# One attention-and-FFN kernel: x loaded already transposed and normalised in that layout

## The chip, the cores and the metric

One core of a Trainium2 chip runs the whole program. The metric is the device time of one execution in microseconds; the figure quoted for a kernel is the median of its runs. Engines are named as in the profile: PE is TensorE, DVE VectorE, ACT ScalarE, POOL GpSimd, SP the engine that issues the DMAs here. Each takes its own instructions strictly in the order in which the program gives them, and waits on semaphores.

## What is computed

Two sandwich blocks on x of 8 x 512 x 1024 (batch, position, feature), float32: attention with 8 heads of 64 over its layer-normalised input, then a 1024 x 1024 linear layer with a routed low-rank part. Cut to what matters:

```
x = x + layernorm(attn(layernorm(x)))
x = x + layernorm(ffn(layernorm(x)))

attn:  qkv = x @ w_qkv.T + b_qkv            # (b, 512, 1536): q, k, v
       scores = einsum('bhfc,bhtc->bhft', k, q), masked where f > t with -10000
       vals = softmax over f, times v
       out = vals @ w_o.T + b_o
ffn:   hidden @ W.T + b + (x @ A[:r].T @ B[:, :r].T of the best of 4 ranks by a gate)
layernorm(x) = (x - mean(x)) / sqrt(var(x) + 1e-5), over the 1024 features
```

Only the first layernorm and what feeds the q, k and v projections is touched.

## The kernel before

Matrix products that matter to accuracy are done in split form: an operand is rounded to a high part (names ending in h, written by ACT) and a low part (names ending in l, written by DVE as the difference), and a product is three matmuls: high by high, high by low, low by high.

The program has two phases, attention and output; each is written out engine by engine. In the attention phase the weights wh and wl stay in SBUF, and a loop runs over batches 0 to 6, with batch 7 written out behind it. A batch has ten slots, h = 0 to 9. In slot h stand the scores of head h (L797; for heads 3 to 6, the list AHEAD, at the end of the slot before), its masking and maxima (L504 on DVE) and exponentials (L662 on ACT), the normalisation of its probabilities (L381 on POOL), and, one slot later, the transposes of these (L816 on PE) with their high and low copies (p_hi L629 on ACT, p_lo L471 on DVE); in slot h + 2 come the values (L841 on PE), then their sum (L530) and store. Projections fill the rest: q and k for two heads at a time ("pair", 24 matmuls of 512 columns), v for 128 positions at a time. The table BETWEEN (L104) writes by hand which projections stand in which of the two parts of a slot; FIRST and SECOND are halves of the eight blocks of 128 features.

A projection needs x with features on the partitions, xTh and xTl, eight blocks of 128 x 512. Before the change they are made one batch ahead, in slots 4 to 6: SP loads four tiles of 128 positions (L286), DVE takes mean and variance (L452), POOL normalises a tile in place (L368), PE transposes it in 8 pieces of 128 x 128 into two PSUM banks (L756), ACT evicts the high part (x_hi, L622) and DVE the low one (x_lo, L464). These 32 transposes share the two banks ps_j with the projections. After them come k and q of pair 0 and pair 1 of the next batch, in slots 6 to 9.

SP issues every DMA: the x tiles, the duplicate of k to the other half of the partitions (dup_k, L288), the store of a head's values (L294). PE waits for xTl before pair 0 (L780), for the bank to be free (L750), for the exponentials of the head before (L807), for p_lo (L821, L844).

Of the kernel before, what the change touches and what calls it, by code (L numbers as in the profile page):

```python
# [16 lines left out]
ALU = mybir.AluOpType  # L17
ACT = mybir.ActivationFunctionType
AX = mybir.AxisListType
F32 = mybir.dt.float32  # L20
# [57 lines left out]
def attention_phase(nc, x, wqkvT, bqk, bv, valsT, vals_stored, ps_o, W, woT, bo, wagT, BT):  # L78
# [24 lines left out]
    WHOLE, FIRST, SECOND = range(KD), range(KD // 2), range(KD // 2, KD)  # L103
    BETWEEN = [  # L104
# [18 lines left out]
    EARLY = [("x", t, g) for t in range(NT) for g in range(2)] + [("k", 0), ("q", 0), ("k", 1), ("q", 1)]  # L123
    NOW = [("v", 0), ("v", 1), ("v", 2), ("v", 3), ("k", 2), ("q", 2), ("k", 3), ("q", 3)]

    with ExitStack() as ctx:
# [10 lines left out]
        xs = sb("xs", [P, 3, D], F32)  # L137
# [28 lines left out]
        nmean = sb("nmean", [P, 2], F32)  # L166
        mhalf = sb("mhalf", [P, 1], F32)
# [25 lines left out]
        xn_ready = sem("xn_ready")  # L193
        t_full = [sem(f"t_full{i}") for i in range(2)]
# [40 lines left out]
        xf = x.rearrange("b s d -> (b s) d")  # L235
        vf = valsT.rearrange("b c t -> (b c) t")
# [12 lines left out]
        def x_tile(t, b):  # L249
            if t == 3 and isinstance(b, int) and b == 0:  # L250
                return x3
            return xs[:, t % 3, :]

        def x_bank(t, g, b):

            return (ps_t if isinstance(b, int) and b == 0 and t % 2 else ps_j)[g]
# [7 lines left out]
        def j_index(entry, b):  # L264

            if entry in EARLY:
                return 20 * b + EARLY.index(entry)
            return 20 * b + len(EARLY) + NOW.index(entry)

# [3 lines left out]
        def j_uses(entry, b):  # L273

            return 10 * b + j_index(entry, 0) // 2 + 1
# [8 lines left out]
        def _(sp):  # L284
            def load_x(t, b):
                sp.dma_start(x_tile(t, b)[:, :], xf[bass.ds(b * S + t * P, P), :]).then_inc(x_landed[t], 16)  # L286
# [20 lines left out]
            def body(b, last):  # L307
                if not last:

                    sp.wait_ge(j_lo, j_index(("x", 3, 1), b) + 1)  # L310
                    for t in range(3):
                        load_x(t, b + 1)
                for h in range(SLOTS):
                    if h >= 2:
# [3 lines left out]
                    if h == 4 and not last:  # L318

                        sp.wait_ge(j_full[1], j_uses(("x", 0, 1), b + 1))  # L320
                        load_x(3, b + 1)
# [26 lines left out]
            for t in range(3):  # L348
                load_x(t, 0)
            load_x(3, 0)  # L350
# [16 lines left out]
        def _(pool):  # L367
            def layernorm(t, b):  # L368

                n, q = 4 * b + t, t % 2  # L370
                pool.wait_ge(mv_ready, n + 1)
                pool.tensor_tensor(var_eps[:, q:q + 1], mv[:, q, 1:2], eps[:, :], ALU.add).then_inc(ve_done, 1)
                pool.tensor_tensor(nmean[:, q:q + 1], mv[:, q, 0:1], mone[:, :], ALU.mult)
                pool.wait_ge(ve_done, n + 1)
                pool.tensor_tensor(rstd[:, q:q + 1], var_eps[:, q:q + 1], mhalf[:, :], ALU.pow)
                pool.drain()
                at = x_tile(t, b)[:, :]
                pool.tensor_scalar(at, at, nmean[:, q:q + 1], rstd[:, q:q + 1], ALU.add, ALU.mult)\
                    .then_inc(xn_ready, 1)

            def normalise(h, b):  # L381
# [1004 lines left out]
```

## Time and profile before

| what | value |
|---|---|
| median of 3 runs | 1586.88 us (1586.53 to 1590.59) |
| profiled execution, span | 1589.1 us |
| PE busy in the span | 1500.4 us, 94% |
| DVE, ACT, POOL busy | 975.6, 675.2, 557.7 us |
| mean granted clock of PE | 0.982 |

The attention phase ends at about 921 us of the span, the output phase follows. A batch of the loop takes about 110 us (43.14 to 814.79 us for seven). The clock is given as a share of 2.4 GHz; 0.5 is 1.2 GHz. PE's matmuls overlap, so the pitch from one start to the next is what they cost in a row, and the duration shown is longer.

### The profile page before, as it was taken

Reading aid. Unit: us, or ns where it says so; the run is one execution under the profiler, and the core shown is the slowest. Engines: PE = TensorE matmul, PEld = TensorE weight load, DVE = VectorE, ACT = ScalarE, POOL = GpSimd, SP = SyncE. Lnnn points to the kernel's source line nnn. Section 1 sums busy time; section 2 is a strip of 40 time slices with the busy share of each in tenths; the row PEclk is TensorE's granted clock in tenths of the full one; section 3 lists DMA queues with packets and bytes.
Section 4 is the critical chain, followed back from the end, with each engine's and each line's share of the span. In section 5 each row is a group of like instructions: output and inputs, shape, how many; then the busy total and the mean of one; then the engine's idle time right before and its main releaser. Section 6 shows DMA issues by size and latency. Waiting matters only on the chain. (4 is left out here: it accounts for less than half of the span.)

```text
span 1589.1 us, 24982 instructions
## 1 busy us (share of the span) xinstructions
PE 1500.4 (94%) x8032; PEld 1316.6 (83%) x8032; DVE 975.6 (61%) x2133; ACT 675.2 (42%) x1464; POOL 557.7 (35%) x1099
## 2 busy tenths in 40 slices
PE   7989999989999999999899769999999999999996
PEld 5878878878878788788787569999999999999996
DVE  7475574665665655755745666666666666666663
ACT  5354364464553653644544543333333333333331
POOL 2232431432332323314312444443333334433333
PEclk9999999999999999999999889999999999999998
DMA  6121112012022111120110632211111111111210
GB/s 225 54 54 42 54 40 76 20 36 76 20 53 59 50 40 59 36 79 17 40 37 24 205 97 67 66 66 64 61 64 60 64 62 64 59 64 66 66 60 40
DMA packets 45774, 98.72 MB, mean 62 GB/s; under 512 B 4912, under 2 KB 21296, under 8 KB 45744
## 3 DMA queue, kind: packets, MB, share of 16 engines
q1 hardware_dynamic: 45744, 98.35, 20.2%
q8 instruction: 16, 0.26, 0.1%
q14 instruction: 14, 0.11, 0.0%
HBM read 56.39 MB, written 25.17 MB: 51 GB/s over the span
## 5 line engine op out<-in xcount | busy, mean ns | idle before, releaser
L1312 PE MATMUL ps_f<-wagh,x2Th 128*128 128x364 f32 x768 | 256.1, 333 | 4.4 <-DVE f L1174 2.9
L1312 PE MATMUL ps_f<-wagl,x2Th 128*128 128x364 f32 x768 | 253.9, 331 | 0.0
L1312 PE MATMUL ps_f<-wagh,x2Tl 128*128 128x364 f32 x768 | 253.3, 330 | 0.0
L782 PE MATMUL ps_o<-xTh,wh 128*128 128x512 f32 x504 | 202.2, 401 | 5.5 <-DVE xTl L468 5.5
L782 PE MATMUL ps_o<-xTh,wl 128*128 128x512 f32 x504 | 198.5, 394 | 0.0
L782 PE MATMUL ps_o<-xTl,wh 128*128 128x512 f32 x504 | 198.0, 393 | 0.0
L1312 PEld LDWEIGHTS ps_f<-wagh,x2Th 128*128 128x128 f32 x768 | 146.5, 191 | 6.8 <-issue 5.0
L1312 PEld LDWEIGHTS ps_f<-wagl,x2Th 128*128 128x128 f32 x768 | 145.7, 190 | 1.3
L1312 PEld LDWEIGHTS ps_f<-wagh,x2Tl 128*128 128x128 f32 x768 | 145.2, 189 | 0.0
L392 POOL TENSOR_SCALAR pr<-pr,rden 128x128 f32<-128x128 f32 (+3 forms) x256 | 136.5, 552 | 0.0
L385 POOL TENSOR_TENSOR cw<-wm,cnt 128x4 f32<-128x4 f32 x64 | 12.7, 199 | 346.1 <-ACT pr L668 346.1
L668 ACT ACTIVATE pr<-ps_s,nm 128x128 f32<-128x128 f32 (+3 forms) x256 | 130.5, 520 | 0.1
L1045 POOL TENSOR_TENSOR var_eps<-mv,eps 128x1 f32<-128x1 f32 x95 | 19.0, 200 | 309.0 <-DVE mv L1108 309.0
L1159 DVE TENSOR_TENSOR x2Tl<-ps_x,x2Th 128x512 fp32r<-128x512 f32 x64 | 42.7, 688 | 128.5 <-ACT x2Th L1233 128.3
L474 DVE TENSOR_TENSOR PTl<-ps_t,PTh 128x512 fp32r<-128x512 f32 (+1 forms) x192 | 109.2, 596 | 19.6 <-ACT PTh L632 16.8
L1213 ACT ACTIVATE zf<-f,shift,rstd 128x512 f32<-128x512 f32 x64 | 48.7, 809 | 168.2 <-POOL shift L1049 168.2
L632 ACT ACTIVATE PTh<-ps_t 128x512 fp32r<-128x512 f32 (+1 forms) x192 | 94.3, 527 | 56.4 <-PE ps_t L837 53.7
L665 ACT ACTIVATE wm<-nm,masked 128x3 f32<-128x3 f32 x64 | 19.0, 296 | 233.0 <-DVE nm L524 233.0
L782 PEld LDWEIGHTS ps_o<-xTh,wh 128*128 128x128 f32 x504 | 95.9, 190 | 24.6 <-DVE xTl L468 6.8
L782 PEld LDWEIGHTS ps_o<-xTh,wl 128*128 128x128 f32 x504 | 95.5, 190 | 21.0
L782 PEld LDWEIGHTS ps_o<-xTl,wh 128*128 128x128 f32 x504 | 96.0, 190 | 18.4
L519 DVE TENSOR_REDUCE nm<-ps_s 128x1 f32<-128x128 f32 (+3 forms) x256 | 107.7, 482 | 2.2
(152 smaller groups left out, 3519.4 us busy)
## 6 DMA issues: line engine op xcount, KB each, us to landing
kst<-kst SPq DMA_DIRECT2D x64, 256.0 KB, 3.5
xt<-in_x SPq DMA_DIRECT2D x32, 512.0 KB, 4.1
out<-outs SPq DMA_DIRECT2D x32, 512.0 KB, 3.0
xs<-in_x SPq DMA_DIRECT2D x31, 512.0 KB, 4.4
valsT<-vt SPq DMA_DIRECT2D x64, 128.0 KB, 2.3
vraw<-valsT SPq DMA_DIRECT2D x32, 256.0 KB, 4.3
raw<-in_wqkvT SPq DMA_DIRECT2D x12, 512.0 KB, 5.9
wag_raw<-in_wagT SPq DMA_DIRECT2D x8, 546.0 KB, 6.0
```

The source lines that it names most:

```text
L385: pool.tensor_tensor(cw[:, q, :], wm[:, q, :], cnt[:, :], ALU.mult).then_inc(cw_done, 1)
L392: last = pool.tensor_scalar(at, at, rden[:, q, i:i + 1], 1.0, ALU.mult, ALU.mult)
L474: dve.tensor_tensor(PTl[:, o:o + n], ps_t[g % 2][:, 0:n], PTh[:, o:o + n].bitcast(F32), ALU.subtract).then_inc(t_lo, 1)
L519: last = dve.tensor_reduce(nm[:, q, i:i + 1], ps_s[:, S_OFF[i]:S_OFF[i] + (i + 1) * P], AX.X, ALU.max, negate=True)
L632: act.activation(PTh[:, o:o + n], ps_t[g % 2][:, 0:n], ACT.Copy).then_inc(t_hi, 1)
L665: act.activation(wm[:, q, 0:3], nm[:, q, 0:3], ACT.Exp, bias=masked[:, :])
L668: last = act.activation(pr[:, q, S_OFF[i]:S_OFF[i] + n], ps_s[:, S_OFF[i]:S_OFF[i] + n], ACT.Exp, bias=nm[:, q, i:i + 1], accum_out=acc[:, ...
L782: last = pe.matmul(ps[:, :], w[:, k, c:c + P], xT[:, k, :], start=(k == 0 and w is wh and xT is xTh), stop=(k == KD - 1 and w is wl), skip ...
L1045: pool.tensor_tensor(var_eps[:, c:c + 1], mv[:, c, 1:2], eps[:, :], ALU.add)
L1159: dve.tensor_tensor(x2Tl[:, 4 * g:4 * g + 4, :], ps_x[:, g, :].rearrange("p (k t) -> p k t", k=4), x2Th[:, 4 * g:4 * g + 4, :].bitcast(F32 ...
L1213: return act.activation(out_, in_, ACT.Identity, scale=rstd[:, c:c + 1], bias=shift[:, c:c + 1])
L1312: last = pe.matmul(ps_f[:, g, 0:GW], a[:, k, :], w[:, k, cols], start=(k == 0 and a is x2Th and w is wagh), stop=False, skip_group_check=True)
```

## The change

The host hands over x a second time, transposed within each batch (xT). Batch 0 is made as before, by transposes on PE. For batches 1 to 7:

- SP loads the four tiles of 128 positions two at a time, for statistics alone; DVE takes them after slots 0 and 1, POOL makes -mean and 1/sqrt(var + eps) as columns of a small tile ms.
- SP stores ms as two rows of 512 floats to DRAM, waits for that, and loads them back broadcast to all partitions (mr).
- SP loads xT in eight chunks of 128 features x 512 positions (four places). Each is centred by POOL (one tensor_tensor), scaled by POOL (chunks 0 to 3) or DVE (4 to 7), copied to its high part by ACT and to its low part by DVE.
- PE no longer transposes x in the loop; the projections of k and q of pairs 0 and 1 move up into slots 5 to 9 in smaller pieces, and k of pair 0 waits for each chunk's low part by itself.

Cut to its core:

```diff
     WHOLE, FIRST, SECOND = range(KD), range(KD // 2), range(KD // 2, KD)
+    THIRDS = range(0, 3), range(3, 5), range(5, KD)
     BETWEEN = [
...
-        ([("q", 3, 0, WHOLE)], [("x", 0, 1, WHOLE)]),
-        ([("x", 1, 1, WHOLE)], [("x", 2, 1, WHOLE)]),
-        ([("x", 3, 1, WHOLE)], [("k", 0, 1, WHOLE)]),
-        ([("q", 0, 1, FIRST)], [("q", 0, 1, SECOND), ("k", 1, 1, FIRST)]),
-        ([("k", 1, 1, SECOND)], [("q", 1, 1, FIRST)]),
-        ([("q", 1, 1, SECOND)], []),
+        ([("q", 3, 0, WHOLE)], []),
+        ([("k", 0, 1, FIRST)], [("q", 0, 1, FIRST)]),
+        ([("k", 0, 1, SECOND)], [("q", 0, 1, SECOND)]),
+        ([("k", 1, 1, FIRST)], [("k", 1, 1, SECOND)]),
+        ([("q", 1, 1, THIRDS[0])], [("q", 1, 1, THIRDS[1])]),
+        ([("q", 1, 1, THIRDS[2])], []),
     ]
...
+        room = sb("x_room", [P, 3, D], F32)
+        xc = room[:, 0:2, :].rearrange("p a (b t) -> p (a b) t", b=2)
+        mr = room[:, 2, :].rearrange("p (q t) -> p q t", q=2)
...
         @block.sync   # body
+                    if h == 1 and not last:
+                        for t in range(2, NT):
+                            sp.wait_ge(mv_ready, NT * (b + 1) + t - 1)
+                            load_tile(t, b + 1)
+                    if h == 2 and not last:
+                        sp.wait_ge(xn_ready, NT * (b + 1) + NT)
+                        with nc.allow_non_contiguous_dma(reason="a column of each tile becomes a row"):
+                            sp.dma_start(norms.rearrange("(q t p) -> p q t", q=2, t=NT), ms[:, :, :])\
+                                .then_inc(norms_stored, 16)
+                        for k in range(NC):
+                            load_chunk(k, b + 1)
+                        sp.wait_ge(norms_stored, 16 * (b + 1))
+                        sp.dma_start(room[:, 2, :], norms.partition_broadcast(P)).then_inc(norms_landed, 16)
+                    if h == 5 and not last:
+                        for k in range(NC, KD):
+                            sp.wait_ge(x_lo, x_count(k - NC, b + 1))
+                            load_chunk(k, b + 1)
                     if h >= 2:
                         store_vals(h - 2, b)
...
         @block.gpsimd
+            def centre(k, b):
+                if k == 0:
+                    pool.wait_ge(norms_landed, 16 * b)
+                pool.wait_ge(chunk_landed[k % NC], 16 * (KD // NC) * (b - 1) + 16 * (k // NC + 1))
+                pool.tensor_tensor(x_chunk(k), x_chunk(k), mr[:, 0, :], ALU.add).then_inc(centred, 1)
+
+            def scale(k, b):
+                pool.wait_ge(centred, KD * (b - 1) + k + 1)
+                pool.tensor_tensor(x_chunk(k), x_chunk(k), mr[:, 1, :], ALU.mult).then_inc(chunk_ready, 1)
...
                 for h in range(NH):
                     if h == 5 and not last:
-                        layernorm(3, b + 1)
+                        centre(4, b + 1)
+                        centre(5, b + 1)
                     normalise(h, b)
-                    if h < 3 and not last:
-                        layernorm(h, b + 1)
+                    if h < 2 and not last:
+                        norm(2 * h, b + 1)
+                        norm(2 * h + 1, b + 1)
+                    if h in (2, 3) and not last:
+                        for act_on in (centre, scale):
+                            act_on(2 * h - 4, b + 1)
+                            act_on(2 * h - 3, b + 1)
+                    if h == 5 and not last:
+                        centre(6, b + 1)
+                        centre(7, b + 1)
...
         @block.vector
+            def scale(k, b):
+                dve.wait_ge(centred, KD * (b - 1) + k + 1)
+                dve.tensor_tensor(x_chunk(k), x_chunk(k), mr[:, 1, :], ALU.mult).then_inc(chunk_ready, 1)
+
+            def chunk_lo(k, b):
+                dve.wait_ge(x_hi, x_count(k, b))
+                dve.tensor_tensor(xTl[:, k, :], x_chunk(k), xTh[:, k, :].bitcast(F32), ALU.subtract).then_inc(x_lo, 1)
...
                     if h < NH:
                         scores_max(h, b)
+                    if h == 6 and not last:
+                        for k in range(6, KD):
+                            chunk_lo(k, b + 1)
                     lows(h, 0, b, last)
...
                         for g in range(2):
                             p_lo(h - 1, g, b)
+                    if h == 4 and not last:
+                        for k in range(2):
+                            chunk_lo(k, b + 1)
+                    if h == 5 and not last:
+                        for k in (4, 5):
+                            scale(k, b + 1)
                     if h < NH:
                         reciprocal(h, b)
...
-                        if h < 3:
-                            layernorm_stats(h, b + 1)
+                        if h < 2:
+                            layernorm_stats(2 * h, b + 1)
+                            layernorm_stats(2 * h + 1, b + 1)
+                        if h == 4:
+                            for k in range(2, NC):
+                                chunk_lo(k, b + 1)
+                        if h == 5:
+                            for k in (4, 5):
+                                chunk_lo(k, b + 1)
+                            for k in (6, 7):
+                                scale(k, b + 1)
...
         @block.scalar
                     if h < NH and not bare:
                         exps(h, b)
+                    if h == 6 and not last:
+                        for k in range(6, KD):
+                            chunk_hi(k, b + 1)
...
         @block.tensor   # project
                 for k in ks:
-                    if (kind, p) == ("k", 0) and k in (0, 4):
-
-                        pe.wait_ge(j_lo, j_index(("x", 3, k // 4), b) + 1)
+                    if (kind, p) == ("k", 0) and not (isinstance(b, int) and b == 0):
+                        pe.wait_ge(x_lo, x_count(k, b))
```

How the queues read where slot 5 ends and slot 6 begins. Rows of the kernel before carry its own line numbers, rows of the changed one those of the changed file. DVE before, from the third p_lo of head 4 (PTl) over the maxima of head 6 (hold to nm) to the low part of the last tile of x (xTl):

```order
L474 TENSOR_TENSOR PTl<-ps_t,PTh 128x256 [waits t_hi]
...
L510 MEMSET hold 1x1 [waits s_done,held]
L514 COPY_PREDICATED ps_s<-maskf,masked 128x3x128
L516 COPY_PREDICATED ps_s<-maskf,masked 128x128
...
L519 TENSOR_REDUCE nm<-ps_s 128x1 x3
L524 TENSOR_SCALAR nm<-nm 128x3 [waits max_done]
...
L468 TENSOR_TENSOR xTl<-ps_o,xTh 128x4x128 [waits j_hi]
```

DVE after, the same place: the scale of chunks 6 and 7 (x_room) and their low parts (xTl) stand on either side of the maxima:

```order
L551 TENSOR_TENSOR xTl<-x_room,xTh 128x512 [waits x_hi]
...
L547 TENSOR_TENSOR x_room<-x_room 128x512 [waits centred]
...
L592 MEMSET hold 1x1 [waits s_done,held]
L596 COPY_PREDICATED ps_s<-maskf,masked 128x3x128
L598 COPY_PREDICATED ps_s<-maskf,masked 128x128
...
L601 TENSOR_REDUCE nm<-ps_s 128x1 x3
L606 TENSOR_SCALAR nm<-nm 128x3 [waits max_done]
```

The maxima of head 6 stand behind two operations that wait for POOL (centred); before, nothing of x stood ahead of them. POOL before, from the normalisation of the last tile of x over head 5 (cw to Dw) to head 6:

```order
L378 TENSOR_SCALAR xs<-xs,nmean,rstd 128x1024
...
L385 TENSOR_TENSOR cw<-wm,cnt 128x4 [waits exp_done]
L387 TENSOR_TENSOR den<-cw,acc 128x4 [waits cw_done]
L389 TENSOR_TENSOR wn<-wm,rden 128x4 [waits rden_ready]
L392 TENSOR_SCALAR pr<-pr,rden 128x128
L392 TENSOR_SCALAR pr<-pr,rden 128x256
L392 TENSOR_SCALAR pr<-pr,rden 128x384
L392 TENSOR_SCALAR pr<-pr,rden 128x512
L399 TENSOR_TENSOR Dw<-ident,wn 128x384 [waits wt_ready,wn_done]
```

POOL after, from the reciprocal's use in head 5 (wn) to the centring of chunks 6 and 7 (their places are those of chunks 2 and 3, hence chunk_landed2 and 3):

```order
L446 TENSOR_TENSOR wn<-wm,rden 128x4 [waits rden_ready]
L449 TENSOR_SCALAR pr<-pr,rden 128x128
L449 TENSOR_SCALAR pr<-pr,rden 128x256
L449 TENSOR_SCALAR pr<-pr,rden 128x384
L449 TENSOR_SCALAR pr<-pr,rden 128x512
L456 TENSOR_TENSOR Dw<-ident,wn 128x384 [waits wt_ready,wn_done]
L432 TENSOR_TENSOR x_room<-x_room 128x512 [waits chunk_landed2]
L432 TENSOR_TENSOR x_room<-x_room 128x512 [waits chunk_landed3]
```

The normalisation of the tile stood ahead of head 5; the centring of the last two chunks stands behind it.

## Rows read from the trace of the kernel before

**Rows 1.** Busy time by engine, batch 3 and its x stretch (window, length, engines, clock, DMA).

```profile
374.29:484.25 109.96, 105.77 (x561) 89.33 (x561) 66.73 (x145) 55.15 (x140) 35.35 (x80) 1.00 0.17 48
434.43:453.01 18.58, 14.43 (x94) 11.29 (x93) 17.57 (x39) 12.43 (x31) 8.42 (x18) 1.00 0.27 71
```

**Rows 2.** Timeline of PE, end of slot 2 and slot 3 (start, duration, instruction).

```profile
412.00 1.44 PE L810 MATMUL ps_s<-kst,qst 128*128 128x128 f32 x8
413.27 0.38 PE L837 MATMUL ps_t<-ident,pr 128*128 128x128 f32 x2
...
413.67 0.39 PE L782 MATMUL ps_o<-xTh,wh 128*128 128x512 f32 x1
...
416.38 0.39 PE L852 MATMUL ps_v<-PTh,v 128*128 128x512 f32 x1
...
418.05 1.03 PE L837 MATMUL ps_t<-ident,pr 128*128 128x128 f32 x8
418.84 0.48 PE L782 MATMUL ps_o<-xTh,wh 128*128 128x512 f32 x1
```

**Rows 3.** Groups of instructions (shapes, count | busy us, mean ns | idle before).

```profile
L1069 POOL TENSOR_TENSOR outs<-x,zf 128x512 f32<-128x512 f32 x64 | 81.3, 1292 | 30.8 <-ACT zf L1213 30.8
...
L595 DVE TENSOR_TENSOR wl<-raw,wh 128x1024 fp32r<-128x1024 f32 x12 | 14.2, 1221 | 2.4 <-ACT wh L728 2.3
...
L728 ACT ACTIVATE wh<-raw 128x1024 fp32r<-128x1024 f32 x12 | 12.3, 1059 | 3.9 <-DMA raw<-in_wqkvT 3.9
```

**Rows 4.** Timeline of DVE in batch 3, slots 1 to 5.

```profile
401.33 1.27 DVE L459 BATCH_NORM_STATS2 stats<-xs 128x6 f32<-128x512 f32 x2
...
411.67 1.29 DVE L474 TENSOR_TENSOR PTl<-ps_t,PTh 128x512 fp32r<-128x512 f32 x2
...
436.70 1.29 DVE L474 TENSOR_TENSOR PTl<-ps_t,PTh 128x512 fp32r<-128x512 f32 x2
...
439.50 0.62 DVE L514 COPY_PREDICATED_SCALAR ps_s<-maskf,masked 128x384 f32 x1
...
442.12 0.17 DVE L524 TENSOR_SCALAR nm<-nm 128x3 f32<-128x3 f32 x1
```

**Rows 5.** Timelines of DVE and POOL at one place of the output phase.

```profile
1211.12 1.30 DVE L1147 TENSOR_TENSOR us<-um,us 128x64 fp32r<-128x64 f32 x1
1212.35 1.78 DVE L1165 TENSOR_TENSOR vl<-vraw,vh 128x512 fp32r<-128x512 f32 x1
...
1211.05 2.54 POOL L1060 TENSOR_TENSOR x<-xt,z 128x512 f32<-128x512 f32 x2 [1.01 <-ACT z L1213]
```

**Rows 6.** Timeline of ACT, head 5's exponentials and what follows them.

```profile
442.33 0.30 ACT L665 ACTIVATE wm<-nm,masked 128x3 f32<-128x3 f32 x1 [1.73 <-DVE nm L524]
...
444.44 0.21 ACT L668 ACTIVATION_READ_ACCUMULATOR pr<-ps_s,nm 128x1 f32 x1
444.68 0.59 ACT L677 ACTIVATE vt<-ps_v 64x512 f32<-64x512 f32 x1
445.30 1.08 ACT L632 ACTIVATE PTh<-ps_t 128x512 fp32r<-128x512 f32 x2
```

**Rows 7.** Timeline of POOL, first and last step of head 5's normalisation.

```profile
448.07 0.20 POOL L389 TENSOR_TENSOR wn<-wm,rden 128x4 f32<-128x4 f32 x1 [0.29 <-DVE rden L528]
...
450.26 0.83 POOL L399 TENSOR_TENSOR Dw<-ident,wn 128x384 fp32r<-128x384 f32 x1
```

**Rows 8.** Busy time by engine where PE had idled: PEclk is the eighth figure.

```profile
16.00:18.00 2.00, 0.00 (x0) 0.00 (x0) 1.97 (x3) 2.00 (x4) 0.00 (x0) 0.89 0.00 0
18.00:24.00 6.00, 5.49 (x13) 4.33 (x14) 6.00 (x6) 4.25 (x5) 0.00 (x0) 0.50 0.78 242
...
926.00:928.90 2.90, 2.90 (x7) 2.32 (x8) 2.38 (x1) 2.90 (x4) 2.86 (x7) 0.50 0.83 294
```

**Rows 9.** DMA issues (count, KB each, median us from issue to landing).

```profile
kst<-kst SPq DMA_DIRECT2D x64, 256.0 KB, 3.5
...
bqk_s<-in_bqk SPq DMA_DIRECT2D x1, 4.0 KB, 8.3
```

More of the change, by code:

```diff
@@ L193, in attention_phase @@
         xn_ready = sem("xn_ready")
+        x_full = [sem(f"x_full{i}") for i in range(2)]
+        x_hi = sem("x_hi")
+        x_lo = sem("x_lo")
+        tile_landed = [sem(f"tile_landed{i}") for i in range(2)]
+        chunk_landed = [sem(f"chunk_landed{i}") for i in range(NC)]
+        norms_stored = sem("norms_stored")
+        norms_landed = sem("norms_landed")
+        centred = sem("centred")
+        chunk_ready = sem("chunk_ready")
         t_full = [sem(f"t_full{i}") for i in range(2)]
@@ L247, in raw_chunk, with x_tile, x_bank @@
             return raw[:, n % RAW, :] if n < KD else raw[:, n % RAW, :].rearrange("p (k c) -> p k c", k=2)
[L249 to L256, printed above, removed]
+        def x_tile(t):
+            return x3[:, :] if t == 3 else room[:, t, :]
+        def x_bank(t, g):
+            return (ps_t if t % 2 else ps_j)[g]
         def pair_bank(kind, p, b):
@@ L571, in body @@
                         first_attention_out()
-                    if h == 5 and not last:
-                        layernorm_stats(3, b + 1)
                     if h >= 2:
@@ L686, in first_vals_high, with highs @@
                 act.activation(W.vh[:, :, :, :], W.vraw[:, :, :, :], ACT.Copy).then_inc(v_first_hi, 1)
-            def highs(h, part, b, last, kinds="qkvx"):
+            def highs(h, part, b, last):
                 for kind, p, row, ks in between(h, part, b, last):
-                    if ks is not FIRST and kind in kinds:
-                        {"q": q_hi, "k": k_hi, "v": v_hi, "x": x_hi}[kind](p, row)
+                    if KD - 1 in ks:
+                        {"q": q_hi, "k": k_hi, "v": v_hi}[kind](p, row)
             def body(b, last):
@@ L706, in body @@
                             p_hi(h - 1, g, b)
+                    if h == 4 and not last:
+                        for k in range(2):
+                            chunk_hi(k, b + 1)
                     if h < NH and bare:
@@ L715, in body @@
                         masked_spread(h - 1, b)
+                    if h == 4 and not last:
+                        for k in range(2, NC):
+                            chunk_hi(k, b + 1)
+                    if h == 5 and not last:
+                        for k in (4, 5):
+                            chunk_hi(k, b + 1)
                     if last and h == 9:
@@ L730, in _ @@
             for t in range(3):
[L731 removed]
+                first_hi(t)
             split_w(0)
[L733 removed]
+            first_hi(3)
             for n in range(1, KD + 2):
@@ L1345, in _, with build @@
             body(NB - 1, True)
-def build(nc, valsT, out, x, wqkvT, bqk, bv, woT, bo, wagT, bf, gb, BT):
+def build(nc, valsT, norms, out, x, xT, wqkvT, bqk, bv, woT, bo, wagT, bf, gb, BT):
     with ExitStack() as room:
```

154 lines of the change are left out of this document (85 added, 69 removed).

## The prediction

> **What bounds the kernel now.** I read the stretches of one middle batch first, then the TensorE timeline inside them, then the queues of VectorE (DVE), ScalarE (ACT) and GpSimd (POOL) at the same place. Batch 3 lasts 109.96 us, from 374.29 to 484.25, and TensorE is busy for 105.77 of them [rows 1]. Nearly all that it loses lies in one stretch, 434.43 to 453.01, where it has work for 14.43 of 18.58 us. That is the stretch in which the 32 transposes of the next batch's x stand; outside it TensorE is the bound and every engine beside it is hidden. So the question is what this stretch costs after the change, and whether a new one opens.
>
> All times below are on the clock of batch 3. The loop runs seven times with a batch behind it, so a difference counts seven times. The last batch and the output phase run the same code as before.
>
> **What the removal gives.** Dense prices come from slots 2 and 3, start to start [rows 2]: scores of a head 1.27 us (412.00 to 413.27), the last pair of its probability transposes with the Dw product 0.40 (to 413.67), twelve projection matmuls 2.71 (413.67 to 416.38), the values of a head 1.67 (to 418.05), the first eight probability transposes 0.79 (to 418.84). The stretch of 18.58 us holds, beside the x transposes, two of each but the projections: 2 x 4.13 = 8.26. The transposes with all that they wait for therefore cost 18.58 - 8.26 = 10.3 us a batch. The projections that are reordered are the same matmuls, so they move time and add none. Seven times 10.3 is 72 us, the most that the change can give: 1515 us.
>
> **What is added, off TensorE.** Durations by the nearest rows: a POOL tensor_tensor of 128x512 takes 1.29 us; DVE's on two SBUF operands 0.6 (half of 1.22 for 1024 columns); ACT's copy 0.55 (half of 1.06) [rows 3]. Gone in return are eight evictions on ACT, eight on DVE and four normalisations on POOL. Engine totals stay far below 110 us; what counts is where each new operation stands in its in-order queue.
>
> **Slot 2.** Statistics now run two tiles at a time after slots 0 and 1, each 1.27 us on DVE for the two halves [rows 4], and with drain and aggregate, an estimate, 1.5. So maxima and exponentials of head 2 are 1.5 us later, and with them p_lo of head 1, now 411.67 to 412.96 [rows 4]: it ends at 414.45, while TensorE wants it from 413.27 on [rows 2]. The Dw product then ends at 414.9 instead of 413.67: +1.2 us.
>
> **Slots 4 and 5, up to chunk 5.** The probability transposes of head 3 end at 434.43. Scores of head 5 follow to 435.7, then the last pair must wait for p_lo, which DVE finishes at 437.99 [rows 4]: to 438.4. DVE then does x_lo of chunks 0 and 1 (437.95 to 439.15), the reciprocal and p_lo's last part (439.65), and x_lo of chunks 2 and 3. Here POOL is in its four scalings of head 4. In the output phase DVE's L1147, 64 columns on two SBUF operands, takes 1.30 us, up to the end of the POOL operation that began 0.07 us before it, and L1165 behind it 1.78 us [rows 5]: the two engines take turns, a whole instruction each. I apply that to every POOL operation that reads SBUF; the other end of this price is no blocking at all. Taking turns, chunk 3 is ready at 441.65. Maxima of head 5 take 2.79 us (439.50 to 442.29 [rows 4]) and end at 444.35; exponentials 2.32 (442.33 to 444.65 [rows 6]), 446.75. ACT then evicts the values and p_hi (0.6 + 1.1 [rows 6]), DVE the values' sum and p_lo up to 449.45, scale of chunks 4 and 5 to 450.65, and only now the reciprocal of head 5 (450.8). TensorE meanwhile does k0's first half to 442.3, values, transposes, q0's first half and scores of head 6 to 448.8, the last pair behind p_lo to 449.9, chunk 4 when x_lo has it (452.0) and chunk 5 (453.1) to 453.85. From 434.43 that is 19.4 us for 12.6 us of work: 6.8 us of waits.
>
> By the Trainium skill's page "SBUF — State Buffer", section "Who interferes with whom", a DVE instruction with two SBUF inputs contends with a GpSimd instruction that reads SBUF, whoever issues first holding the port for the whole instruction. The output-phase rows agree for tensor_tensor on both sides; no row of the kernel before shows it for POOL's scalings. By the page the sum is the one below; if the scalings were exempt it would be 2.1 us a batch less, 1669.
>
> **Slot 6, the chain that decides.** POOL's queue has centre of chunks 6 and 7 behind the whole normalisation of head 5; DVE's queue has scale of 6 and 7 ahead of the maxima of head 6; ACT has x_hi of 6 behind the exponentials of head 6; DVE has x_lo of 6 behind those maxima; TensorE has the rest of k0 behind x_lo of 6, and values, transposes and q0 behind that. So, from the reciprocal at 450.8: normalisation 3.0 us (448.07 to 451.09 [rows 7]) and two turns given to x_lo of 4 and 5 (1.2) and the gaps between, 455.2; two centres 2.55, 457.75; two scales, the first held by the second centre, 458.95; maxima 2.79, 461.75; exponentials 2.32 and the hand-over, 464.15; x_hi 0.55 and x_lo 0.6, 465.35. TensorE came to chunk 6 at 453.85: it stands for **11.5 us**, with nothing else that it may do.
>
> **Behind it.** The rest of the batch is 26.5 us of work at dense prices. In slots 7 and 8 head 7's softmax chain again starts only with its own scores, and two p_lo come late: 1.7 + 0.8 = 2.5 us. The clock: after an idle stretch of TensorE the granted clock falls to 0.5, the 1.2 GHz level; at the start it is 0.89 mean while TensorE does nothing (16 to 18) and 0.50 through 18 to 24, with TensorE busy for 5.49 us; at 926 it is 0.50 for 2.9 us after an idle gap [rows 8]. Half speed over 2.9 to 5.9 us of work loses 1.5 to 3 us; I take 2.1. A stall of 11.5 us is longer than any idle gap in those stretches, so I expect the fall in each batch; the low end is none.
>
> **Sum.** Waits 1.2 + 6.8 + 11.5 + 2.5 + 2.1 = 24.1 us a batch, against 10.3 taken out: +13.8, times seven +97 us. The profiled execution is 1589.1 us, which gives 1686; the median of the runs is 2.2 us below it, so **1684 us**.
>
> SP's queue: loads of chunks 4 to 7 wait for x_lo of 0 to 3 and go out at about 438.6 to 441.7; SBUF transfers of 256 KB land in 3.5 us [rows 9], before POOL is free for centre of 4 (443.7), so they cost nothing. Chunks 0 to 3 and the norms have slot 2 and 3 to land; POOL's eight operations there (10.3 us) lie between normalisations that wait for exponentials and end at 434.4, when head 4's reciprocal is still 5 us away. Cover gone, they would be added to head 4's chain.
>
> **Rivals.**
> (a) The same chain, without blocking between DVE and POOL (0.9 us in slot 4, 1.7 in slots 5 and 6) and without the fall of the clock (2.1): 13.8 - 4.7 = 9.1 a batch, 1651 us. For it: POOL's scalings were never seen beside such a DVE operation.
> (b) The norms come late. SP stores 1024 single floats, waits until they have landed, then broadcasts them, and only then stores values of head 0 and duplicates k of heads 4 and 5. It starts at about 405.3. The smallest pieces in the trace, bqk's rows, took 8.3 us [rows 9], behind 512 KB loads. It decides from about 15 us of store and landing on, since k's copy must go out by 421 to be there for head 4's scores at the end of slot 3 (418.84 and 24 matmuls, 424.3) [rows 2]; at 20 us it costs 5 us more a batch: 1719.
> The Trainium skill ("DMA: Bandwidth & Descriptors", "Rules for kernel authors") says that a non-contiguous last dim becomes one descriptor per element and should be rearranged. No run here shows the price of such a store; it speaks for (b).
> (c) Even. If chunks 6 and 7 reach TensorE without the big wait (and so without the fall of the clock), 24.1 - 13.6 = 10.5 remain against 10.3: 1588 us.
> (d) Faster. TensorE stays the bound in slots 4 to 9 as it is in slots 0 to 3, because the chunks are ready a slot ahead of their use, and only slot 2 costs: 7 x (10.3 - 1.2) = 64 us less, 1523 us. It decides where all waits together stay under 10.3 us a batch. For it: each engine beside TensorE is idle a third of the batch or more [rows 1]. Against it: the queues' order, which leaves chunk 6 no other way than through head 6's exponentials. That the change does not take the transposes out at all is excluded by the order: none is left in the loop.
>
> **How the numbers follow.** Forecast (1684, own range 1655 to 1712) 0.66; (a) 0.17; (b) 0.07; (c) 0.04; (d) 0.06. Slower by over 0.3%, about what a measurement of this kernel can tell from no change, 0.90; within it 0.04; faster 0.06. The range, 1640 to 1712, takes in (a), the low end of the clock and of the blocking, and half of the late norms.
>
> **What would show it.** In the profile after: batches of about 123 to 124 us; no transposes of x behind the first batch; one gap of TensorE of about 11 us a batch, before the seventh chunk of k0, released by DVE's xTl; DVE idle before that on POOL's centre, for some 3 to 5 us; the granted clock at 0.5 behind that gap; DVE's x_lo of chunks 2 to 5 longer than 0.65 us. It is wrong if that gap is under 3 us, if a batch is shorter than 110 us, or if the longest wait is on a DMA.

## The result and the profile after

The changed kernel takes **1697.69 us** (median of 4 runs, 1690.11 to 1700.21) against 1586.70 for four runs of the kernel before: ratio 1.0686, 95% interval 1.066 to 1.0713. The forecast was 1684, its range 1640 to 1712. From the page of the profiled execution (span 1694.8 us), busy time and share of each engine, and TensorE's granted clock in 40 slices:

```profile
PE 1512.3 (89%) x7808; PEld 1314.6 (78%) x7808; DVE 1015.7 (60%) x2161; ACT 675.6 (40%) x1464; POOL 646.9 (38%) x1155
PEclk9998988988988988988988997999999999999998
```

Most 8s among the first 23 digits of the clock row stand where a batch's waits have pulled the clock down. Batch 3 now runs from 419.58 to 546.14; its stretches answer to [rows 1] (window, length, PE busy, clock, DMA share, GB/s):

```profile
419.58:546.14 126.56, 108.12 (x530) 0.91 0.26 62
419.58:480.40 60.82, 60.20 (x307) 1.00 0.34 76
480.40:504.57 24.17, 17.54 (x74) 0.82 0.27 76
504.57:514.38 9.81, 0.00 (x1) 0.50 0.00 0
514.38:519.20 4.82, 4.82 (x13) 0.50 0.00 0
519.20:546.14 26.94, 25.55 (x141) 0.99 0.22 54
```

Up to the probability transposes of head 3 (480.40) the batch is nearly as it was: 60.82 us against 60.14 from 374.29 to 434.43. Nearly all the loss of this batch, 15.9 of 16.6 us, stands behind that. The seven batches take 124.9 to 126.7 us, 125.9 on average, against 110.2 before: 15.7 us times seven is 110 of the 111 us. TensorE's timeline shows where it stands (start, duration, instruction; in brackets the idle time ahead of it and who ended it):

```profile
459.18 0.44 PE L948 MATMUL ps_t<-ident,pr 128*128 128x128 f32 x2 [0.46 <-DVE PTl L556]
...
482.37 1.55 PE L921 MATMUL ps_s<-kst,qst 128*128 128x128 f32 x8 [1.73 <-ACT pr L771]
486.68 0.69 PE L948 MATMUL ps_t<-ident,pr 128*128 128x128 f32 x2 [2.76 <-DVE PTl L556]
...
502.03 0.50 PE L893 MATMUL ps_o<-xTh,wh 128*128 128x512 f32 x1 [2.13 <-DVE xTl L551]
...
514.38 0.79 PE L893 MATMUL ps_o<-xTh,wh 128*128 128x512 f32 x1 [9.81 <-DVE xTl L551]
...
534.47 0.44 PE L948 MATMUL ps_t<-ident,pr 128*128 128x128 f32 x2 [1.06 <-DVE PTl L556]
```

The long one, 9.81 us, is k0's seventh chunk; in all batches it is 9.7 to 10.3 us. The chain to it, from DVE, POOL and ACT in order of time, is the one that the prediction laid out:

```profile
500.19 0.17 DVE L610 RECIPROCAL rden<-den 128x4 f32<-128x4 f32 x1
500.61 3.01 POOL L449 TENSOR_SCALAR pr<-pr,rden 128x128 f32<-128x128 f32 x4
504.37 2.48 POOL L432 TENSOR_TENSOR x_room<-x_room 128x512 f32<-128x512 f32 x2
505.66 2.34 DVE L547 TENSOR_TENSOR x_room<-x_room 128x512 f32<-128x512 f32 x2 [3.08 <-POOL x_room L432]
508.83 1.68 DVE L601 TENSOR_REDUCE nm<-ps_s 128x1 f32<-128x128 f32 x4
512.30 0.69 ACT L771 ACTIVATE pr<-ps_s,nm 128x512 f32<-128x512 f32 x1
512.96 1.15 ACT L730 ACTIVATE xTh<-x_room 128x512 fp32r<-128x512 f32 x2
513.63 1.29 DVE L551 TENSOR_TENSOR xTl<-x_room,xTh 128x512 fp32r<-128x512 f32 x2 [2.92 <-ACT xTh L730]
```

Reciprocal of head 5, its scalings, the centres of 6 and 7, DVE's scale (which waits 3.08 us and then runs beside the second centre), the maxima of head 6, its exponentials, x_hi, x_lo. From the reciprocal to TensorE's matmul it takes 14.2 us; the prediction had 450.8 to 465.35, 14.55.

### The profile page after: what moved, and what is told of

The parts are those of the page before. It is cut to its first block and busy times, and to the rows that moved or that the text cites. A ratio compares the mean times of both kernels' runs of the same rounds, so it can differ in the third digit from the quotient of the medians.

```text
span 1694.8 us, 24812 instructions
## 1 busy us (share of the span) xinstructions
PE 1512.3 (89%) x7808; PEld 1314.6 (78%) x7808; DVE 1015.7 (60%) x2161; ACT 675.6 (40%) x1464; POOL 646.9 (38%) x1155
## 2 busy tenths in 40 slices
DMA packets 62127, 117.12 MB, mean 69 GB/s; under 512 B 13200, under 2 KB 29584, under 8 KB 62096
## 5 line engine op out<-in xcount | busy, mean ns | idle before, releaser
L893 PE MATMUL ps_o<-xTh,wh 128*128 128x512 f32 x504 | 216.6, 430 | 86.9 <-DVE xTl L551 84.3
L893 PE MATMUL ps_o<-xTh,wl 128*128 128x512 f32 x504 | 209.4, 416 | 0.0
L893 PE MATMUL ps_o<-xTl,wh 128*128 128x512 f32 x504 | 209.2, 415 | 0.0
L893 PEld LDWEIGHTS ps_o<-xTh,wh 128*128 128x128 f32 x504 | 101.5, 201 | 114.8 <-DVE xTl L551 93.3
L449 POOL TENSOR_SCALAR pr<-pr,rden 128x128 f32<-128x128 f32 (+3 forms) x256 | 151.1, 610 | 0.0
L948 PE MATMUL ps_t<-ident,pr 128*128 128x128 f32 x640 | 94.5, 279 | 39.4 <-DVE PTl L556 35.8
L948 PEld LDWEIGHTS ps_t<-ident,pr 128*128 128x128 f32 x640 | 75.7, 142 | 59.6 <-DVE PTl L556 49.2
L893 PEld LDWEIGHTS ps_o<-xTh,wl 128*128 128x128 f32 x504 | 102.2, 203 | 23.7
L893 PEld LDWEIGHTS ps_o<-xTl,wh 128*128 128x128 f32 x504 | 102.2, 203 | 18.9
L556 DVE TENSOR_TENSOR PTl<-ps_t,PTh 128x512 fp32r<-128x512 f32 (+1 forms) x192 | 109.0, 596 | 10.3 <-ACT PTh L735 7.6
```

The lines of the kernel that those rows point to most:

```text
L449: last = pool.tensor_scalar(at, at, rden[:, q, i:i + 1], 1.0, ALU.mult, ALU.mult)
L556: dve.tensor_tensor(PTl[:, o:o + n], ps_t[g % 2][:, 0:n], PTh[:, o:o + n].bitcast(F32), ALU.subtract).then_inc(t_lo, 1)
L893: last = pe.matmul(ps[:, :], w[:, k, c:c + P], xT[:, k, :], start=(k == 0 and w is wh and xT is xTh), stop=(k == KD - 1 and w is wl), skip ...
L948: last = pe.transpose(ps_t[bank][:, at - o:at - o + P], pr[:, h % 2, S_OFF[i] + j * P:S_OFF[i] + (j + 1) * P], ident[:, :])
```

## Experiments

Medians, each ratio against runs of the kernel before on the same chip; "a batch" is the difference to the changed kernel (1697.69) divided by seven. The kernel before took 1586.7 to 1589.0 us beside them, a spread worth 0.3 us a batch.

| kernel | us | ratio to before, 95% | a batch |
|---|---|---|---|
| centres of 6 and 7 first | 1677.54 | 1.0563 (1.0546 to 1.0581) | -2.9 |
| x_hi, x_lo of 6 and 7 first | 1677.48 | 1.0558 (1.054 to 1.0575) | -2.9 |
| both | 1660.65 | 1.045 (1.0429 to 1.0471) | -5.3 |
| norms not waited for | 1678.79 | 1.0576 (1.0556 to 1.0595) | -2.7 |
| both, norms in halves | 1643.9 | 1.0346 (1.0326 to 1.0365) | -7.7 |
| work in the windows | 1585.28 | 0.9989 (0.9974 to 1.0005) | -16.1 |
| TensorE kept busy | 1685.93 | 1.0623 (1.0599 to 1.0646) | -1.7 |
| windows, early statistics | 1576.8 | 0.9919 (0.9895 to 0.9943) | -17.3 |
| early statistics alone | 1674.44 | 1.0541 (1.0526 to 1.0557) | -3.3 |
| windows, early statistics, norms whole | 1560.7 | 0.9826 (0.9813 to 0.9839) | -19.6 |
| the row above, and values first in slot 7 | 1562.01 | 0.9829 (0.9816 to 0.9843) | -19.4 |
| clamp left out | 1679.44 | 1.0569 (1.0552 to 1.0585) | -2.6 |

### The links of the chain

```
 POOL: if h == 5 and not last:
-          centre(4, b + 1); centre(5, b + 1)
+          for k in range(4, KD): centre(k, b + 1)
       normalise(h, b)
       ...
-      if h == 5 and not last:
-          centre(6, b + 1); centre(7, b + 1)
```

> Edit: POOL centres chunks 6 and 7 ahead of head 5's normalisation, behind chunks 4 and 5, instead of behind it. Theory (the wait of TensorE at k0's seventh chunk is set by the order in the queues, and POOL's place for the two centres is one link of it): DVE's scale of chunks 6 and 7 no longer waits for POOL (3.1 us in batch 3 of the changed kernel) nor shares with it (2.34 us instead of 1.28), so the wait shrinks by about 4 us a batch, from 9.8 to some 6, and the time falls by 28 us to about 1670. Rival 1 (chunks 6 and 7 land late, the transfer sets the wait): the centres stand before head 5's sums and hold them up; no gain, 1698 or more. Rival 2 (the softmax of head 6 is late for reasons of its own): the wait stays near 9.8 us, time within 5 us of 1698.

```
 DVE:  scores_max(h, b)
-      if h == 6 and not last:
-          for k in range(6, KD): chunk_lo(k, b + 1)
       ...
       for k in (6, 7): scale(k, b + 1)          # end of slot 5
+      for k in (6, 7): chunk_lo(k, b + 1)
 ACT:  exps(h, b)
-      if h == 6 and not last:
-          for k in range(6, KD): chunk_hi(k, b + 1)
       ...
-      for k in (4, 5): chunk_hi(k, b + 1)       # end of slot 5
+      for k in range(4, KD): chunk_hi(k, b + 1)
```

> Edit: ACT's x_hi and DVE's x_lo of chunks 6 and 7 stand at the end of slot 5, ahead of exponentials and maxima of head 6, instead of behind them; POOL's order as in the changed kernel. Theory: maxima and exponentials of head 6 (2.8 and 2.3 us, with the hand-overs 5.2) come out of the chain to the seventh chunk: the wait falls from 9.8 to about 5 us, the time by 33 us to about 1665. Rival (TensorE then waits for head 6's softmax instead, since scores of head 7 and the transposes of head 6 need it 5 us later): gain under 10 us, 1688 or more, with a wait at scores of head 7 on ACT's exponentials.

> Edit: both of the above together. Theory: the two links add up: 4 + 5 us a batch; the seventh chunk is ready about 1.5 us after TensorE comes to it, TensorE's long idle stretch is gone and with it the fall of the granted clock behind it (1.3 us a batch or more): about 10 us a batch, 1626 us. Rival 1 (the links overlap: the one hides the other): the gain is that of the larger alone, 1665. Rival 2 (without the long wait even with the kernel before, as the prediction's case (c) says): 1588.

The wait at the seventh chunk with the first edit, with the second, and the waits of slots 5 and 6 with both:

```profile
503.18 0.79 PE L890 MATMUL ps_o<-xTh,wh 128*128 128x512 f32 x1 [6.75 <-DVE xTl L548]
```

```profile
505.31 0.79 PE L889 MATMUL ps_o<-xTh,wh 128*128 128x512 f32 x1 [4.61 <-DVE xTl L551]
```

```profile
489.39 0.63 PE L886 MATMUL ps_o<-xTh,wh 128*128 128x512 f32 x1 [1.83 <-DVE xTl L548]
502.39 0.44 PE L941 MATMUL ps_t<-ident,pr 128*128 128x128 f32 x2 [2.93 <-DVE PTl L553]
```

In batch 3 the waits did what the theory says: 9.81 falls to 6.75 (6 expected; 5.4 to 5.9 in the other batches), to 4.61 (5 expected; 4.2 to 5.8 in the others), and with both edits the seventh chunk is not waited for in batch 3, and for 0.5 to 1.3 us in the six others. Both links are shown. The gains are not: 20 us each instead of 28 and 33, and 37 instead of 70. What the first wait gives up, the next takes. With both edits, the last pair of head 5's transposes waits 2.93 us for p_lo, because DVE's and ACT's work of head 6 now stands behind the chunks, not ahead of them. DVE's maxima (first instruction of heads 4 to 7) show the pace of these slots:

```profile
464.14 0.62 DVE L593 COPY_PREDICATED_SCALAR ps_s<-maskf,masked 128x384 f32 x1
478.25 0.62 DVE L593 COPY_PREDICATED_SCALAR ps_s<-maskf,masked 128x384 f32 x1
492.87 0.61 DVE L593 COPY_PREDICATED_SCALAR ps_s<-maskf,masked 128x384 f32 x1
505.95 0.62 DVE L593 COPY_PREDICATED_SCALAR ps_s<-maskf,masked 128x384 f32 x1
```

14.1, 14.6 and 13.1 us a head. So the chunk work lengthens a loop of DVE and ACT (maxima, exponentials, evictions, chunks, next maxima), and moving it within the loop brings little. That became the next theory.

### The way of the norms

```
 SP:   sp.wait_ge(xn_ready, NT * (b + 1) + NT)
-      sp.dma_start(norms..., ms[:, :, :]).then_inc(norms_stored, 16)
+      sp.dma_start(room[:, 2, :], bo.partition_broadcast(P)).then_inc(norms_landed, 16)
       for k in range(NC): load_chunk(k, b + 1)
-      sp.wait_ge(norms_stored, 16 * (b + 1))
-      sp.dma_start(room[:, 2, :], norms.partition_broadcast(P)).then_inc(norms_landed, 16)
```

> Leaves out the store of means and deviations and the wait for it: an input row is broadcast in their place at the start of slot 2, so x is centred and scaled with wrong numbers. Theory (the norms' way through memory, 18 us from the last statistics, makes POOL's eight chunk operations late, these head 3's sums, these DVE's maxima of head 4): centring starts 5.7 us earlier, maxima of head 4 about 1.8 us earlier; the wait of scores of head 5 on exponentials (1.7 us) goes: 1.8 to 2.5 us a batch, 1680 to 1685 us. Rival 1 (the prediction's: the way costs nothing because it is hidden beside slots 2 and 3): within 3 us of 1698. Rival 2 (it delays all of slots 4 and 5, some 4 us a batch): 1670.

In the changed kernel, the store's issue row, the centre of chunks 0 and 1 on POOL, head 3's reciprocal on DVE, and what the two waits sum to (over all batches, times, longest):

```profile
norms<-ms SPq DMA_DIRECT2D x7, 4.0 KB, 11.0
```

```profile
468.61 2.55 POOL L432 TENSOR_TENSOR x_room<-x_room 128x512 f32<-128x512 f32 x2 [5.69 <-DMA x_room<-norms]
474.14 0.18 DVE L610 RECIPROCAL rden<-den 128x4 f32<-128x4 f32 x1 [3.42 <-POOL den L444]
```

```profile
POOL x_room L432 <- DMA x_room<-norms: 36.2, 7, 6.1
DVE rden L610 <- POOL den L444: 22.0, 9, 3.4
```

Without the store (the broadcast then also goes out ahead of the chunk loads) POOL centres 43.3 us into batch 3 instead of 49.0, neither wait is left there, and 18.9 us come back: 2.7 a batch. The theory stands; rival 1, the prediction's own claim, falls. Two versions that leave nothing out agree. With both links moved and the first half stored a slot earlier (SP stores means and deviations of tiles 0 and 1 behind slot 0):

> Edit: the kernel with both links moved (centres of 6 and 7 first, their x_hi and x_lo first), and the means and deviations stored in two halves, the first right behind slot 0's statistics, so that only half of the small pieces is still under way when the broadcast could start. Nothing is left out. Theory (the norms' way holds up POOL's chunk operations, and through head 3's sums all of slots 4 to 6): the landing falls from 11.0 to some 6 us, centring starts about 5 us earlier, the time falls from 1661 by most of the 19 us which the run without the wait gave: 1645 to 1650. Rival 1 (with the long wait gone the loop of slots 4 to 6 has its own pace, which no earlier start changes): within 3 us of 1661. Rival 2 (the pieces' landing time does not go with their number): as the kernel with both links, 1661.

1643.9, 16.8 less than without the halves. And on the changed kernel the statistics alone, all in slot 0:

```
 DVE:  scores_max(h, b)
+      if h == 0 and not last:
+          layernorm_stats(0, b + 1); layernorm_stats(1, b + 1)
       ...
-      if h < 2:
-          layernorm_stats(2 * h, b + 1); layernorm_stats(2 * h + 1, b + 1)
+      if h == 0:
+          layernorm_stats(2, b + 1); layernorm_stats(3, b + 1)
```

> Edit: the changed kernel with only its statistics moved: all four in slot 0 (two behind maxima of head 0, two at the slot's end), the norms stored whole and broadcast from slot 1 on; the queues of slots 2 to 9 as in the changed kernel. Theory (two separate prices of the statistics' place: the wait in slot 2, 1.1 us a batch, and the late norms, 2.7 us by the run without the wait): 3.8 us a batch, 27 us, 1671. Rival 1 (slot 2's wait has another cause and stays): 1679. Rival 2 (the gain of the run without the wait came from wrong numbers or fewer packets, not from the time of landing): 1690 or more.

1674.44: slot 2 has no wait any more and POOL does not wait for the norms, 3.3 us a batch of the 3.8 expected.

### The clamp beside POOL

```
 DVE:  last = dve.tensor_reduce(nm[...], ps_s[...], AX.X, ALU.max, negate=True)
-      last.then_inc(max_done, 1)
-      dve.wait_ge(max_done, H + 1)
-      dve.tensor_scalar(nm[:, q, 0:3], nm[:, q, 0:3], -MASKED, None, ALU.min).then_inc(nm_ready, 1)
+      last.then_inc(nm_ready, 1)
```

> Leaves out one operation of the changed kernel: DVE's clamp of the maxima (128x3, one SBUF operand), with the hand-over before it; the queues stay. Theory (the clamp, 0.17 us elsewhere, is held for 1.2 and 1.0 us at heads 4 and 5 until POOL's tensor_tensor beside it ends, and lies on the chain to the seventh chunk): exponentials of heads 4, 5 and 6 start 1.3, 1.1 and 0.3 us earlier, 2.5 us a batch, 1680 us. Rival 1 (not on the chain, or POOL holds the next operation instead): only the operation itself, 0.3 us a head, 1690 to 1693. Rival 2 (no effect at all): 1698.

The clamp of head 4 in the changed kernel, and POOL's centres and scalings beside it:

```profile
478.75 1.20 DVE L606 TENSOR_SCALAR nm<-nm 128x3 f32<-128x3 f32 x1
```

```profile
477.39 2.54 POOL L432 TENSOR_TENSOR x_room<-x_room 128x512 f32<-128x512 f32 x2
```

The clamp of head 6, which has no such neighbour:

```profile
510.55 0.17 DVE L606 TENSOR_SCALAR nm<-nm 128x3 f32<-128x3 f32 x1
```

384 numbers take 1.20 us, where the same instruction takes 0.17 in head 6 and in head 3 (463.04), and it ends at 479.95, when POOL's second centre ends (479.93): it stood until POOL was done. Left out, it gives 18.3 us; three operations a batch of some 0.3 us with their hand-over, an estimate, would have given 6. It was held, and it lay on the path.

### The clock

```
 PE:   if (kind, p) == ("k", 0) and not first batch:
+          if k == 6:
+              pe.wait_ge(vals_ready, 1 + 8 * (b - 1) + 4)
+              for i in range(40):
+                  pe.matmul(ps_v[:, :], wh[:, 0, 0:P], xTh[:, 0, :], start=True, stop=True)
           pe.wait_ge(x_lo, x_count(k, b))
```

> Edit: the changed kernel, and 40 further matmuls of 128x512 (9 us at full clock) into the values' PSUM bank, which is free there, ahead of TensorE's wait for the seventh chunk; their result is overwritten. Everything else as in the changed kernel. Theory (the long idle stretch makes the granted clock fall to its 1.2 GHz level, and the work behind it runs at half speed: the six matmuls 2.72 instead of 1.36 us, the values 2.81 instead of 1.67): with TensorE busy through the stretch the clock stays up, 2.5 us a batch come back although 40 matmuls are added: about 1681 us. Rival 1 (the chain of DVE and ACT sets the time behind the stretch too, so a faster TensorE waits later): 1690 to 1698. Rival 2 (the fall has another cause): the clock falls all the same and the time is 1698 or more.

Forty matmuls more, and 11.8 us less. At the end of the added work TensorE still waits a moment, but the next matmuls run at 0.23 us each, not 0.43:

```profile
510.39 0.50 PE L897 MATMUL ps_o<-xTh,wh 128*128 128x512 f32 x1 [0.34 <-DVE xTl L551]
510.72 0.39 PE L897 MATMUL ps_o<-xTl,wh 128*128 128x512 f32 x1
510.95 0.39 PE L897 MATMUL ps_o<-xTh,wl 128*128 128x512 f32 x1
```

From that matmul to the start of k1 it takes 8.5 us, in the changed kernel 10.8 (514.38 to 525.21). So in batch 3 the fall behind the long wait costs 2.4 us; over the seven batches (9.8 to 11.1 us against 8.5) it costs some 16 us, an estimate. A part of the gain is lost again, since in five of the seven batches chunk 6 is still waited for, 0.3 to 2.3 us, behind the added work.

### The work in the windows, and a version faster than both

If the loop of DVE and ACT is the bound, the chunk work has to go where these engines wait for each other. The edit in words, by engine:

```
 ACT:  + slot 4, ahead of exps(4): chunk_hi(0), chunk_hi(1)   # as soon as q3 has read the chunk
       + slot 4, behind p_hi(3): chunk_hi(2), chunk_hi(3), q_hi(3) last
       + slots 5, 6: vals_lo_part and p_hi ahead of exps(h); chunk_hi(4 to 7) in slot 5
 DVE:  + slot 4, behind scores_max(4): chunk_lo(0), chunk_lo(1), reciprocal(4); q_lo(3) last
       - scale(4 to 7)
 POOL: + scale(4 to 7); scale(6), scale(7) between den(5) and rden(5)
 SP:   + chunks 4, 5 loaded in slot 4; norms in halves
```

> Edit, on top of the norms in halves: the work on the chunks is put where its engine waits anyway. POOL does all scalings; ACT copies chunks 0 and 1 ahead of exponentials of head 4 (each as soon as q3 has read that chunk), and does the values and p_hi of heads 3 to 5 ahead of exponentials of heads 5 and 6; DVE does x_lo of 0 and 1 and the reciprocal while it waits for exponentials of head 4; q3's evictions come last in slot 4; chunks 4 and 5 are loaded a slot earlier. Theory (with both links moved TensorE is held in slots 4 to 6 by one chain: DVE's maxima, ACT's exponentials, then the evictions and the chunk work on both, then the next maxima, 14 us a head against 9.6 us of TensorE's work): the chunk work leaves that chain, a head takes 10 to 11 us, slots 4 to 6 end about 9 to 12 us earlier than with both links: 1575 to 1600 us, about the kernel before or a little under it. Rival (the engines are full in these slots, whatever the order): above 1640.

1585.28, the same as before. Maxima of heads 4 to 7 now follow each other at 13.1, 11.1 and 10.1 us:

```profile
434.09 0.62 DVE L605 COPY_PREDICATED_SCALAR ps_s<-maskf,masked 128x384 f32 x1
447.20 0.62 DVE L605 COPY_PREDICATED_SCALAR ps_s<-maskf,masked 128x384 f32 x1
458.26 0.61 DVE L605 COPY_PREDICATED_SCALAR ps_s<-maskf,masked 128x384 f32 x1
468.37 0.62 DVE L605 COPY_PREDICATED_SCALAR ps_s<-maskf,masked 128x384 f32 x1
```

So the engines were not full; where the chunk work stands was the cost. The edit bundles order, the loads a slot earlier and four scalings moved from DVE to POOL, and what each of these is worth was not measured. Moving the statistics too (as above) and chunks 0 to 3 wholly beside head 4's exponentials:

> Edit, on top of the kernel with the windows: all four statistics stand in slot 0 (two behind maxima of head 0, two at the slot's end), so the norms go to memory a slot earlier; POOL centres and scales chunks 0 and 1 ahead of head 2's normalisation; x_hi and x_lo of chunks 0 to 3 all stand beside exponentials of head 4; chunks 4 to 7 are loaded in slot 4. Nothing is left out. Theory (what the kernel with the windows still loses is the norms' landing, which in its first batches makes scores of head 5 wait and the granted clock fall, 112 instead of 108 us, and the two late statistics in slot 2, 1.1 us): every batch at 106 to 108 us, 1555 to 1572, 1 to 2% under the kernel before. Rival 1 (what is left is the engines' own chain in slots 4 to 8): 1580 to 1587. Rival 2 (POOL now stands in the way of heads 0 to 2): slower than 1590.

1576.8, above the expected range and under rival 1, and in the profiled execution the batches fall into two kinds, 106.1 to 106.4 and 111.7 to 112.6 us. In the long ones DVE waits for the fourth tile of x (batch 3, above); in the short ones it doesn't (batch 5, below):

```profile
391.58 1.29 DVE L536 BATCH_NORM_STATS2 stats<-x_room 128x6 f32<-128x512 f32 x2 [4.43 <-DMA x_room<-in_x]
...
611.64 1.28 DVE L536 BATCH_NORM_STATS2 stats<-x_room 128x6 f32<-128x512 f32 x2
```

SP sends the first half of the norms just behind that tile's load (at 383.1 in batch 3). One store for all four, a slot later, takes it out of the load's way:

> Edit: the kernel with early statistics, but the norms stored in one piece behind the fourth statistics instead of in halves, so that no store of small pieces is under way while the fourth tile of x is loaded. Nothing is left out. Theory (in four of seven batches of the kernel with early statistics the store of the first half held up the fourth tile's load, DVE stood 4.4 us for it, and the last pair of head 0 2.9 us; the other batches took 106.1 to 106.4 us): all seven batches at about 106.3 us, some 24 us less: 1550 to 1562, 1.7 to 2.4% under the kernel before. Rival 1 (the tile's load is late for another reason): the batches of 112 us stay, 1570 to 1585. Rival 2 (the whole store lands too late for POOL's chunk operations ahead of head 2's normalisation): waits of head 2's transposes, 1575 or more.

**1560.7 us, 1.7% under the kernel before**, all seven batches at 106.0 us and none with a fall of the clock. Batch 3 (window, length, PE, weight loads, DVE, ACT, POOL, clock, DMA share, GB/s):

```profile
358.70:464.73 106.03, 102.34 (x530) 85.57 (x529) 69.52 (x145) 55.37 (x140) 52.52 (x92) 1.00 0.31 74
```

> Edit: as the kernel with the norms stored whole, and ACT does values and p_hi ahead of the exponentials in slot 7 too (heads 5 and 6 ahead of exponentials of head 7). Theory (the last pair of head 6 waits 1.0 us for p_lo, which sits behind exponentials of head 7): that wait goes, 7 us less than the kernel with the norms stored whole. Rival (head 7's own probabilities then come later and the transposes in slot 8 wait for them): no gain or a loss of up to 7 us.

Even, 1562.01: the rival. The wait at the last pairs goes, and one at the values comes (9.9 us in all, 8 times):

```profile
PE ps_v L979 <- DVE PTl L569: 9.9, 8, 1.3
```

## Why the prediction was right, and where its sizes were off

**Direction, place and mechanism** came out as put: transposes gone, the sum of new waits larger than their 10.3 us, one long wait a batch at k0's seventh chunk, behind POOL's centre, DVE's scale and head 6's softmax. The link experiments show POOL's centre and head 6's softmax to be links of it. The chain's length was right to 0.4 us; TensorE came to the seventh chunk 4.4 us after the reciprocal and not 3.05, so the wait was 9.8 and not 11.5.

**Slot 2:** +1.1 us measured (459.18 and its neighbours), 1.2 forecast; moving the statistics removes it. **Slots 7 and 8:** 1.7 and 0.7 us measured from start to start (around 534.47 and 541.55), 1.7 and 0.8 forecast.

**Slots 4 and 5 up to chunk 5:** the term that was too small. 24.17 us in batch 3 where 19.4 were forecast. Counted from start to start, the waits there come to 7.3 us, near the 6.8 forecast; most of the rest of the excess is matmuls at the lower clock. Two steps failed:
- "Chunks 0 to 3 and the norms have slot 2 and 3 to land", and POOL's eight operations lie free there. They don't: the norms landed 18 us after POOL had made the last of them (450.7 to 468.6), POOL stood 5.2 us a batch for them, and its chunk operations pushed head 3's sums, DVE's maxima of head 4 and ACT's exponentials. Price 2.7 us a batch. Rival (b) had the right cause and the wrong door: it watched k's copy, which is waited for at all only when the rest gets quicker (0.3 to 1.1 us at head 4's scores in five of seven batches with both links moved). "Cover gone, they would be added to head 4's chain" is what happened.
- "The clock", 2.1 us for one fall. There were two in every batch. In batch 3 it was already down behind the waits of 1.73 and 2.76 us:

```profile
487.88:491.88 4.00, 4.00 (x10) 0.50 1.01 278
```

There twelve projections take 4.87 us against 2.71 [rows 2], in the other batches 4.6 to 5.3. With the six matmuls of chunks 4 and 5 (2.54 us instead of 1.36) and the 2.4 us behind the long wait this makes about 5.7 us in batch 3, an estimate from these three differences. It overlaps with the price of the norms, so the two can't be added.

The run without the store shows what the late norms did to both large terms. Slots 4 and 5 up to chunk 5, and the wait for the seventh chunk, in its batch 3 (window, length, PE busy, clock, DMA share, GB/s):

```profile
472.46:492.35 19.89, 15.76 (x74) 0.91 0.33 92
492.35:503.65 11.30, 0.00 (x1) 0.71 0.00 0
```

19.9 and 11.3 us (the wait is 10.0 to 11.3 in the seven batches), where 19.4 and 11.5 were forecast. So the late norms brought TensorE to the seventh chunk 4.3 us later and the chunk itself 2.8 us later: slots 4 and 5 grew, and the wait behind them shrank. That the 19.9 fits so well is in part luck: a first fall of the clock is still in it (4.13 us for the twelve projections), and the wait that the forecast has at chunk 3 (k0's first half from 438.4 to 442.3, 3.9 us for 2.7 us of work) is not.

**Taking turns:** the direction varied. POOL's scalings beside x_lo took 3.01 and 3.07 us instead of 2.06, while x_lo of chunks 2 and 3 stayed at 1.29 for the two: there POOL waited, and "x_lo of chunks 2 to 5 longer than 0.65 us" is wrong for 2 and 3 (0.64) and right for 4 and 5 (0.75). DVE lost where POOL came first: scale of 6 and 7, 2.34 us for the two, and the clamp, which the prediction did not have. By the Trainium skill's page "SBUF — State Buffer", section "Who interferes with whom", tensor_scalar too can take the port pair that DVE shares with GpSimd, in its two-port modes, and whoever issues first keeps the other out. The trace agrees: the clamp ended with POOL's instruction (479.95 and 479.93). The prediction had applied this only to instructions with two SBUF inputs.

**Rivals.** (a) 1651 supposed no blocking and no fall of the clock; both are in the trace. (c) "without the big wait 1588" is refuted as a price: with the wait down to 1.3 us or less the kernel took 1660.65, since the same queues made the next one. (d) was reachable in part, but only by another order: 1560.7, not 1523.

The sum came within 14 us because errors of both signs met: in batch 3 slots 4 and 5 are 4.8 us over their term, the long wait 1.7 under it, and the late norms stand behind both. On the average of seven batches 15.7 us came where 13.8 were forecast.

## What to carry to other kernels

Work taken off the bound engine and given to idle ones costs what it does to their queues: follow each new operation to the instruction that it stands ahead of, and to who waits for that one. Where two engines hand a softmax to and fro, new work belongs in the windows in which they wait for each other, and its inputs must be there a slot earlier; much the same operations cost 111 us or gained 28 here, by where they stand. When a long wait is removed, price the next one before counting the gain.

## What the runs showed of the hardware

- A store of 1024 single floats, 4 KB, took 11.0 us to land, more than loads of 512 KB (3.7 us for x's tiles). The Trainium skill ("DMA: Bandwidth & Descriptors", "Rules for kernel authors") says that such a last dim becomes one descriptor per element; the trace agrees: the page of the profile counts 13200 packets under 512 B, and 5920 in the run without the seven stores, which is 1040 fewer for each, about one for a float.
- Half of that store, sent behind a tile's load, seems to have held the load up in four of seven batches, where DVE stood 4.4 to 6.0 us for it; with the store moved the wait is gone. In the three other batches the store followed the load just as closely, so what tells them apart stays open.
- Behind two idle stretches of 1.73 and 2.76 us, with 1.55 us of work between them, the granted clock was at its 1.2 GHz level for 4 us of work. It fell too behind 2.77 us alone (batch 1, where the twelve projections took 4.95 us) and behind 1.98 us alone (batch 3 without the store, 4.13 us). Forty useless matmuls in a 9.8 us gap kept it up, and 11.8 us came back.
